# Expert down-projection: the 48-row pieces issued once for two pairs, and the two expert results of a token added by GpSimd

## The chip, the cores and the metric

The kernel runs on one core of one Trainium2 chip. The metric is the device time of one execution in microseconds (us), taken as the median of several runs. All data are fp32.

## What is computed

A transformer block on two sequences of 1024 tokens with 256 channels. First comes gated linear attention with 16 heads in chunks of 64 tokens. Then, on the layer-normed rows `xf`, comes a mixture of eight small experts with two picked for each token, plus a shared network:

```python
probs = softmax(xf @ gate_w.T); top_p, top_i = top_k(probs, 2)
combine = zeros(n, 8); combine[token, top_i] = top_p
h = silu(xf @ expert_fc1[e].T) * (xf @ expert_fc2[e].T)      # 176 hidden columns
y = sum over e of combine[:, e] * (h @ expert_proj[e].T)
shared = (silu(xf @ shared_fc1.T) * (xf @ shared_fc2.T)) @ shared_proj.T   # 704 hidden columns
y = y + sigmoid(xf @ shared_gate_w.T) * shared
out = x + gb * y
```

## The kernel before

Each engine has an instruction stream of its own, and semaphores tie the streams together. The attention runs over four blocks of 512 tokens (about the first 165 us). Then the routing is computed: every token's row is scattered to DRAM (`xs_dram`) twice, sorted by expert, so that each expert's rows fill tiles of 128. There are 39 such tiles (`ETILES`), numbered `i`, and they are handled in 20 pairs `q`. A group is eight tiles or four pairs (`EGRP`, `XPAIRS`); five groups are run, the middle three in a hardware loop.

For a pair, with `u` the tile's place in its group:

- SyncE (`load_tile`, L508) loads the rows into `xt`, which has a place for four pairs. It waits for the transposes of the tile that was there and for its row factors (`goal_ready`).
- The tensor engine (`group`, L1919) does for each even `u`: `up` of tile u (L1877), the transposes of a later tile's rows (`rows_T`, L1861), `hid_T` of the pair before (L1888, L1890), `up` and `rows_T` of tile u+1, and `down` of the pair before.
- `down` multiplies the 176 hidden columns as 128 plus 48. The 128-row parts are L1900. The 48-row part of the even tile sits in array rows 0 to 47 (L1902), that of the odd tile in rows 64 to 111 (L1907). The expert's 48 weight rows for the odd tile have first to be copied to that range by ScalarE (`copy_odd_rows`, L952, into `tail_odd`, two places). The result of tile t of a pair goes into columns 0 to 255 of the PSUM bank `work[t]`.
- The vector engine (`group`, L1419) multiplies the two halves of the hidden layer (`expert_h`, L1389), copies the transposed hidden columns to `hTe` (L1394), makes two row factors (`row_gains`, L1402) and takes the two results out of PSUM with their token weights (`evac_y`, L1409) into `yout`, which has a place for two pairs.
- GpSimd computes where each row goes (`goals`, L667 to L676, a chain of five small operations, two pairs ahead) and scatters the rows to `ys_dram` (`put_rows`, L684), where each token has two rows.

While the last tiles run, the tensor engine starts on the shared network of the last 512 tokens (`shared_up`, L1486 and L1478, then `shared_down`, L1501 and L1515). When all 39 scatters have landed, SyncE loads `ys_dram` back in eight transfers of 512 KB (L526, into `yin`, two for each block of 512 tokens). `combine(n)` on the vector engine then treats two tiles of tokens at a time: it adds the two results of each token (L1454) and adds the sum to `x_sb` (L1460 or L1458). Between these stand the products of the shared network (`mult_up`, L1130 and L1134). For the last four tiles `add_scaled_down` (L1150) adds the shared network's output. SyncE stores each finished tile.

Of the kernel before, what the change touches and what calls it, by code (L numbers as in the profile page):

```python
# [19 lines left out]
ALU = mybir.AluOpType  # L20
# [3 lines left out]
P = 128  # L24
# [153 lines left out]
def adaln_moe(nc, x, cT, wmod, wq, wk, wv, wg1, wg2, bg2, wgate, norm_w, wo,  # L178
              router, e_up, e_down, s_up, s_down, out):
    with ExitStack() as ctx:  # L180
# [40 lines left out]
        def part(n):  # L221
# [17 lines left out]
        tail_odd = xn2[:, 0:2, :]  # L239
# [100 lines left out]
        row_step, row_gain = sq[:, 0, 0:HID], sq[:, 1, :].rearrange("p (a n) -> p a n", a=2)  # L340
        yout = er_pos[:, :, :].rearrange("p a (t c) -> p a t c", t=2)
# [38 lines left out]
            sem("hTp_full"), sem("hTe_ready"), sem("down_full"), sem("y_out"), [sem(f"ys_st{i}") for i in range(4)])  # L380
# [3 lines left out]
        goal_ready, texp1_ready, odd_ready = sem("goal_ready"), sem("texp1_ready"), sem("odd_ready")  # L384
        ld_y = [sem(f"ld_y{i}") for i in range(NBLK)]
# [54 lines left out]
        def _(sp):  # L440
# [80 lines left out]
            for j, s in enumerate(ys_stored):  # L521
                sp.wait_ge(s, 16 * len(range(j, ETILES, 4)))
# [13 lines left out]
        def _(pool):  # L536
# [142 lines left out]
            def put_rows(q):  # L679

                for u in range(min(2, ETILES - 2 * q)):
                    i = 2 * q + u
                    pool.wait_ge(y_out, i + 1)
                    g.indirect_dma_start(out=ys_dram, out_offset=bass.IndirectOffsetOnAxis(ap=goal_u[:, i:i + 1], axis=0),  # L684
                                         in_=yout[:, q % 2, u, :], in_offset=None, bounds_check=TOPK * TOK - 1,
                                         oob_is_err=False).then_inc(ys_stored[i % 4], 16)
# [27 lines left out]
        def _(act):  # L714
# [231 lines left out]
            def odd_rows(q, w, e):  # L946

                act.wait_ge(down_full, q - 1)
                copy_odd_rows(w, e)

            def copy_odd_rows(w, e):
                a.activation(tail_odd[CHUNK:CHUNK + FE1, w % 2, :], edn[0:FE1, 0, bass.ds(e, 1), :].rearrange("p a n -> p (a n)"),  # L952
                             ACT.Copy).then_inc(odd_ready, 1)

            def group(i0, q0, tiles=EGRP, first=False, last=False):
                act.load(ereg, texp_u[0:1, bass.ds(i0, EGRP)])
                e = [act.snap(r, min_val=0, max_val=NE - 1) for r in ereg]
                for u in range(tiles):
                    expert_silu(i0 + u, u)
                    if u % 2:  # L960
                        if first and u < 4:
                            copy_odd_rows(u // 2, e[u])
                        else:
                            odd_rows(q0 + u // 2, u // 2, e[u])
                    if not (last and u + 2 >= tiles):
                        evac_rows(i0 + u + 2, u)

            group(0, 0, first=True)
            with act.Fori(1, ESLOTS // EGRP - 1) as grp:
                group(grp * EGRP, grp * XPAIRS)  # L970
            group(ESLOTS - EGRP, ESLOTS // 2 - XPAIRS, tiles=ETILES - ESLOTS + EGRP, last=True)
# [93 lines left out]
        def _(dve):  # L1065
# [330 lines left out]
            def row_gains(i, u):  # L1396

                if not isinstance(i, int) or i:
                    dve.wait_ge(y_out, i)
                dve.wait_ge(goal_ready, i + 2)  # L1400
                for t in range(2):
                    v.scalar_tensor_tensor(out=row_gain[:, t, :], in0=row_step, scalar=goal[:, (u // 2) % XPAIRS, t, 2:3],  # L1402
                                           in1=rows[:, 0, GB, :], op0=ALU.mult, op1=ALU.add).then_inc(gain_ready, 1)

            def evac_y(i0, q0, u):

                dve.wait_ge(down_full, q0 + u // 2 + 1)
                dve.wait_ge(gain_ready, i0 + u + 2 - u % 2)
                v.scalar_tensor_tensor(out=yout[:, (u // 2) % 2, u % 2, :], in0=work[u % 2][:, 0:HID],  # L1409
                                       scalar=goal[:, (u // 2) % XPAIRS, u % 2, 1:2], in1=row_gain[:, u % 2, :],  # L1410
                                       op0=ALU.mult, op1=ALU.mult).then_inc(y_out, 1)

            def y_slot_free(i0, u):

                n = 16 * (u // 4)
                if not isinstance(i0, int) or i0 or n:
                    dve.wait_ge(ys_stored[u % 4], i0 * 4 + n)

            def group(i0, q0, tiles=EGRP, first=False):  # L1419

                for u in range(0, tiles, 2):
                    expert_h(i0 + u, u)
                    if u or not first:
                        evac_hT(q0 + u // 2 - 1, (u // 2 - 1) % XPAIRS)
                        row_gains(i0 + u - 2 if u else i0 - 2, (u - 2) % EGRP)
# [13 lines left out]
            group(0, 0, first=True)  # L1439
            with dve.Fori(1, ESLOTS // EGRP - 1) as grp:  # L1440
                group(grp * EGRP, grp * XPAIRS)
            group(ESLOTS - EGRP, ESLOTS // 2 - XPAIRS, tiles=ETILES - ESLOTS + EGRP)
            evac_hT(EPAIRS - 1, XPAIRS - 1)
            row_gains(ETILES - 1, EGRP - 2)
            y_slot_free(ESLOTS - EGRP, EGRP - 2)
            evac_y(ESLOTS - EGRP, ESLOTS // 2 - XPAIRS, EGRP - 2)
# [75 lines left out]
        def _(pe):  # L1522
# [369 lines left out]
            def down(i, q, w, e, tiles=2):  # L1892

                pe.wait_ge(hTe_ready, q + 1)
                if isinstance(i, int) and i == 0:
                    pe.wait_ge(hs_ready, FTS * (NBLK - 1) + EARLY_UP)
                at_least(pe, y_out, i, 0)
                for t in range(tiles):
                    main = edn_odd if t else edn[:, 0, :, :]
                    t_.matmul(work[t][:, 0:HID], hTe[:, w % 2, t * P:(t + 1) * P],  # L1900
                              main[:, bass.ds(e[t], 1), :].rearrange("p a n -> p (a n)"), start=True, stop=False)
                ins = t_.matmul(work[0][:, 0:HID], hTe[0:FE1, w % 2, 2 * P:3 * P],  # L1902
                                edn[0:FE1, 1, bass.ds(e[0], 1), :].rearrange("p a n -> p (a n)"), start=False, stop=True)
                if tiles == 2:
                    pe.wait_ge(odd_ready, q + 1)
                    r = slice(CHUNK, CHUNK + FE1)
                    ins = t_.matmul(work[1][:, 0:HID], hTe[r, w % 2, 2 * P:3 * P], tail_odd[r, w % 2, :],  # L1907
                                    start=False, stop=True)
                ins.then_inc(down_full, 1)
# [7 lines left out]
            eprev = [pe.alloc_register(f"expert_prev{u}") for u in range(2)]  # L1917

            def group(i0, q0, before=None, tiles=EGRP, last=False):  # L1919
# [3 lines left out]
                def pair_behind(step, u):  # L1923
                    if u:
                        step(i0 + u - 2, q0 + u // 2 - 1, u // 2 - 1, e[u - 2:u])
                    elif before is not None:
                        step(i0 - 2, q0 - 1, XPAIRS - 1, before)

                for u in range(0, tiles, 2):
# [10 lines left out]
                    pair_behind(down, u)  # L1940
                    if u == 0:
                        for r, v_ in zip(eprev, e[-2:]):
# [23 lines left out]
            down(ETILES - 1, EPAIRS - 1, XPAIRS - 1, previous()[0:1], tiles=1)  # L1966
# [36 lines left out]
```

## Time and profile before

| | us |
|---|---|
| median of 3 runs | 374.45 (374.1 to 374.88) |
| the profiled execution, its own time | 373.3 |
| the profiled execution, its span (first to last instruction) | 371.5 |
| busy: tensor engine / weight loads | 360.9 / 226.3 |
| busy: vector engine / ScalarE / GpSimd | 238.1 / 144.0 / 146.7 |

The granted clock of the tensor engine is full over the whole span. A weight load is listed beside the matmuls because it overlaps them. fp32 matmuls appear as two records each, so a row with x4 stands for two of them. Idle time of an engine matters only where another one waits for it.

### The profile page before, as it was taken

What the parts mean: (1) busy time and instruction counts of PE and PEld (TensorE: products, weight loads), DVE (VectorE), ACT (ScalarE), POOL (GpSimd) and SP (SyncE); (2) the same over time, 40 slices, a digit from 0 to 9 for tenths busy, and PEclk for the clock granted to TensorE, in tenths of its full rate; (3) what the DMA queues carried; (4) which work ended last, traced back from release to release, by engine and by line L of the source; (5) the groups of instructions that cost most, each with busy time, mean ns of one, the idle gap of its engine ahead of it and who ended that gap; (6) DMA issues with size and microseconds to landing.
All of it is one profiled execution on the core that took longest, in us unless ns stands there. A gap on an engine that the chain in (4) does not pass through costs nothing.

```text
span 371.5 us, 10003 instructions
## 1 busy us (share of the span) xinstructions
PE 360.9 (97%) x3871; PEld 226.3 (61%) x3872; DVE 238.1 (64%) x578; ACT 144.0 (39%) x303; POOL 146.7 (39%) x253
## 2 busy tenths in 40 slices
PE   8999999999999989999999999999999999999996
PEld 8445656565766565647744844856666666665464
DVE  4199585998699579764591861165665555556386
ACT  3597638635781613180043311024333333331110
POOL 7706007100710242026270176323666677666200
PEclk9999999999999999999999999999999999999999
DMA  6980300000000000089820082422333333211396
GB/s 194 347 246 11 109 4 3 2 4 4 3 2 5 2 2 4 4 290 278 247 97 19 1 219 88 131 57 88 104 99 112 101 105 90 86 57 45 106 350 230
DMA packets 29901, 36.66 MB, mean 99 GB/s; under 512 B 4567, under 2 KB 26530, under 8 KB 29860
## 3 DMA queue, kind: packets, MB, share of 16 engines
q1 hardware_dynamic: 26452, 27.58, 24.9%
q0 software_dynamic: 3408, 8.51, 6.8%
q8 instruction: 29, 0.48, 0.5%
q14 instruction: 12, 0.10, 0.1%
HBM read 23.31 MB, written 13.68 MB: 100 GB/s over the span
## 4 chain that ended last, share of the span: by engine, by line
PE 87%; ACT 6%; DVE 3%; issue 2%; POOL 2%; DVEq 0%; POOLq 0%; ACTq 0%
PE at_ps L1877 13%; PE work L1486 10%; PE at_ps L1486 8%; PE work L1535 7%; PE at_ps L1501 6%; PE work L1900 5%; PE work L1501 4%; PE work L1902 3%; PE at_ps L1535 3%; PE work L1676 3%; PE at_ps L1861 2%; PE work L1726 2%; PE at_ps L1573 2%; PE o_even L1629 2%; PE at_ps L1726 2%
## 5 line engine op out<-in xcount | busy, mean ns | idle before, releaser
L684 POOL DMA_INDIRECT ys_tokens<-er_pos,goal_u x39 | 42.2, 1082 | 34.1 <-DVE er_pos L1409 26.7
L1877 PE MATMUL at_ps<-arena 128*128 x156 | 54.5, 472 | 0.0
L655 POOL DMA_INDIRECT xs_sorted<-h2tok,pos_u x32 | 31.4, 983 | 37.8 <-DVE pos_u L1031 17.0
L604 POOL TENSOR_TENSOR arena<-arena 128x512 f32<-128x512 f32 x8 | 10.2, 1281 | 76.0 <-DVE arena L1344 76.0
L1877 PEld LDWEIGHTS at_ps<-arena 128*128 128x128 f32 x156 | 26.6, 190 | 14.9 <-issue 6.6
L937 ACT ACTIVATE arena<-at_ps 128x176 f32<-128x176 f32 x39 | 12.4, 318 | 58.8 <-PE at_ps L1877 55.4
L1409 DVE SCALAR_TENSOR_TENSOR er_pos<-work,goal,sq 128x256 f32<-128x256 f32 x39 | 17.1, 480 | 22.0 <-PE work L1907 21.0
L1486 PE MATMUL work<-h2T,sup_sb 128*128 128x512 f32 x56 | 25.8, 600 | 0.2 <-ACT hs L705 0.2
L1389 DVE TENSOR_TENSOR arena<-at_ps,arena 128x176 f32<-128x176 f32 x39 | 13.3, 342 | 18.6 <-ACT arena L937 16.0
L1234 DVE COPY_PREDICATED arena<-causal,at_ps 128x512 f32<-128x512 uint32 x32 | 20.4, 720 | 4.0 <-PE at_ps L1573 4.0
L1501 PE MATMUL at_ps<-sdn_sb,hs 128*128 128x256 f32 x100 | 22.1, 380 | 0.0
L1501 PEld LDWEIGHTS at_ps<-sdn_sb,hs 128*128 128x128 f32 x100 | 18.9, 190 | 3.4 <-issue 1.0
L705 ACT ACTIVATE hs<-at_ps 128x512 f32<-128x512 f32 x9 | 5.4, 597 | 40.2 <-PE at_ps L1486 40.2
L1130 DVE TENSOR_TENSOR hs<-work,hs 128x512 f32<-128x512 f32 x12 | 8.3, 689 | 16.6 <-PE work L1486 16.5
L933 ACT ACTIVATE arena<-at_ps 128x256 f32<-128x256 f32 x39 | 14.9, 384 | 9.7 <-PE at_ps L1861 9.3
L616 POOL TENSOR_TENSOR sq<-sq,sg 128x512 f32<-128x512 f32 x8 | 10.0, 1275 | 21.7 <-issue 21.3
L1402 DVE SCALAR_TENSOR_TENSOR sq<-sq,goal,rows 128x256 f32<-128x256 f32 x40 | 17.4, 477 | 0.0
L1486 PEld LDWEIGHTS work<-h2T,sup_sb 128*128 128x128 f32 x56 | 10.2, 190 | 11.7 <-issue 11.2
L1861 PEld LDWEIGHTS at_ps<-ident,h2tok 128*128 128x128 f32 x78 | 10.9, 141 | 10.0 <-issue 6.1
L809 ACT ACTIVATE gate_pair<-gate_pair 128x512 f32<-128x512 f32 x8 | 4.9, 631 | 26.8 <-DVE gate_pair L1226 26.8
L1535 PE MATMUL work<-hT,wgate_sb 128*128 128x512 f32 x32 | 14.9, 602 | 0.0
L1861 PE MATMUL at_ps<-ident,h2tok 128*128 128x128 f32 x78 | 14.8, 273 | 0.0
(291 smaller groups left out, 823.1 us busy)
## 6 DMA issues: line engine op xcount, KB each, us to landing
h2tok<-xs_sorted SPq DMA_DIRECT2D x40, 131.5 KB
arena<-ys_tokens SPq DMA_DIRECT2D x8, 512.0 KB, 7.5
arena<-in_e_up SPq DMA_DIRECT2D x8, 352.0 KB
x_sb<-in_x SPq DMA_DIRECT2D x4, 512.0 KB, 8.6
out_rows<-x_sb SPq DMA_DIRECT2D x16, 128.0 KB, 3.9
sup_sb<-in_s_up SPq DMA_DIRECT2D x2, 640.0 KB, 4.9
xs_sorted<-state SPq DMA_DIRECT2D x2, 526.0 KB
xs_sorted<-state SPq DMA_DIRECT2D x8, 131.5 KB
```

The source lines that it names most:

```text
L655: g.indirect_dma_start(out=xs_dram, out_offset=bass.IndirectOffsetOnAxis(ap=pos_u[:, k, t:t + 1], axis=0), in_=h2tok[:, t, :], in_offset=N ...
L684: g.indirect_dma_start(out=ys_dram, out_offset=bass.IndirectOffsetOnAxis(ap=goal_u[:, i:i + 1], axis=0), in_=yout[:, q % 2, u, :], in_offs ...
L933: a.activation(xT[:, u % 2, :], at_ps[u % 2][:, 0:KC * P], ACT.Copy).then_inc(xT_ready, 1)
L1234: v.copy_predicated(atm[:, n % 2, j, :], causal[:, :, :].bitcast(U32).rearrange("p r l -> p (r l)"), at_ps[j][:, :]).then_inc(atm_ready, 1)
L1402: v.scalar_tensor_tensor(out=row_gain[:, t, :], in0=row_step, scalar=goal[:, (u // 2) % XPAIRS, t, 2:3], in1=rows[:, 0, GB, :], op0=ALU.mu ...
L1409: v.scalar_tensor_tensor(out=yout[:, (u // 2) % 2, u % 2, :], in0=work[u % 2][:, 0:HID], scalar=goal[:, (u // 2) % XPAIRS, u % 2, 1:2], in ...
L1486: ins = t_.matmul(o[0:m, :], sup_sb[:, k, w, f0:f0 + m], h2T_of[blk][:, k, :], start=(k == 0), stop=(k == KC - 1))
L1501: t_.matmul(o[jj][:, t * HID:(t + 1) * HID], hs[:, f, tk], sdn_sb[:, f, :], start=(t == 0 and f == 0), stop=False, skip_group_check=True)
L1535: ins = t_.matmul(o[:, :], w[:, k, gr * P:(gr + 1) * P], rhs[:, k, :], start=(k == 0), stop=(k == KC - 1))
L1861: ins = t_.transpose(at_ps[u % 2][:, k * P:(k + 1) * P], xt[:, u // 2, u % 2, k * P:(k + 1) * P], ident[:, :])
L1877: ins = t_.matmul(at_ps[2 + u % 2][:, 0:2 * FE], xT[:, u % 2, k * P:(k + 1) * P], eup[:, bass.ds(e, 1), k, :].rearrange("p a n -> p (a n)" ...
L1900: t_.matmul(work[t][:, 0:HID], hTe[:, w % 2, t * P:(t + 1) * P], main[:, bass.ds(e[t], 1), :].rearrange("p a n -> p (a n)"), start=True, s ...
```

## The change

The short matmuls leave `down` and get a function of their own, `down_short`, which issues those of two pairs (four tiles) after the second pair's `down`. To hold both pairs, `work[t]` is used over all 512 columns, the second pair in columns 256 to 511. `down_full` now counts blocks of two pairs. `tail_odd` gets four places. The vector engine takes four results out in one go (`out_rows`), and makes four row factors in one go in the cycle in between; `row_gain` moves to `xn` and has four places. `yout` gets four pairs' places, the additional ones in `h2T`, and each of the eight tiles has its own semaphore. GpSimd's `goals` runs three pairs ahead instead of two. At the end the eight additions of the tokens' two results (128x512 each) move from the vector engine to GpSimd, with a new semaphore `ysum_ready`. The vector engine's share of `combine` for n = 0 to 6 comes after the last product of the shared network, and `add_scaled_down(0)` comes ahead of the last `combine`.

```diff
-        tail_odd = xn2[:, 0:2, :]
+        tail_odd = xn2[:, :, :]
-        row_step, row_gain = sq[:, 0, 0:HID], sq[:, 1, :].rearrange("p (a n) -> p a n", a=2)
-        yout = er_pos[:, :, :].rearrange("p a (t c) -> p a t c", t=2)
+        row_step, row_gain = sq[:, 0, 0:HID], xn
+        yout = [home[:, a, :].rearrange("p (t c) -> p t c", t=2) for home in (er_pos, h2T[:, 0, :, :]) for a in range(2)]
...
-            goals(0)
-            goals(1)
+            for q in range(XPAIRS - 1):
+                goals(q)
             for q in range(EPAIRS):
-                if q + 2 < EPAIRS:
-                    goals(q + 2)
+                if q + XPAIRS - 1 < EPAIRS:
+                    goals(q + XPAIRS - 1)
                 put_rows(q)
+            for n in range(NTILE // 2):
+                if n % 2 == 0:
+                    pool.wait_ge(ld_y[2 * n // TPB], 16 * TOPK)
+                y0, y1 = (yin[:, 2 * n // TPB, k, 2 * n % TPB:2 * n % TPB + 2, :] for k in range(TOPK))
+                g.tensor_tensor(y0, y0, y1, ALU.add).then_inc(ysum_ready, 1)
...
-            def odd_rows(q, w, e):
-                act.wait_ge(down_full, q - 1)
+            def odd_rows(d, w, e):
+                act.wait_ge(down_full, d)
                 copy_odd_rows(w, e)
...
+            def out_rows(i0, d0, u, tiles=4):
+                for n in range(u, u + tiles):
+                    y_slot_free(i0, n)
+                    evac_y(i0, d0, n)
...
                     if u + 1 < tiles:
                         expert_h(i0 + u + 1, u + 1)
-                    for t in range(2):
-                        if u:
-                            y_slot_free(i0, u - 2 + t)
-                            evac_y(i0, q0, u - 2 + t)
-                        elif not first:
-                            y_slot_free(i0 - EGRP, EGRP - 2 + t)
-                            evac_y(i0 - EGRP, q0 - XPAIRS, EGRP - 2 + t)
+                    if u == 4:
+                        out_rows(i0, d0, 0)
+                    elif u == 0 and not first:
+                        out_rows(i0 - EGRP, d0 - XPAIRS // 2, 4)
+                    elif u % 4 == 2:
+                        row_gains(i0 + u - 2, u - 2)
+                        row_gains(i0 + u, u)
...
-                if n % 2 == 0:
-                    dve.wait_ge(ld_y[t // TPB], 16 * TOPK)
-                y0, y1 = (yin[:, t // TPB, k, t % TPB:t % TPB + 2, :] for k in range(TOPK))
-                steps.did(v.tensor_tensor(y0, y0, y1, ALU.add))
-                steps.sync()
+                dve.wait_ge(ysum_ready, n + 1)
+                y0 = yin[:, t // TPB, 0, t % TPB:t % TPB + 2, :]
...
-                for n in {3: (0,), 4: (1, 2, 3), 5: (4, 5, 6)}.get(f, ()):
+                for n in {5: (0, 1, 2, 3, 4, 5, 6)}.get(f, ()):
                     combine(n)
+            steps.sync()
+            add_scaled_down(0)
             combine(NTILE // 2 - 1)
             steps.sync()
-            for jj in range(2):
-                add_scaled_down(jj)
+            add_scaled_down(1)
...
-                at_least(pe, y_out, i, 0)
+                if w % 2 == 0:
+                    at_least(pe, y_out, i, 0)
+                c = slice(w % 2 * HID, w % 2 * HID + HID)
...
+            def down_short(q, w, e, tiles=4):
+                if tiles == 4:
+                    pe.wait_ge(odd_ready, q + 1)
+                else:
+                    pe.wait_ge(odd_ready, q)
+                r = slice(CHUNK, CHUNK + FE1)
+                for a in range(2):
+                    c = slice(a * HID, a * HID + HID)
+                    ins = t_.matmul(work[0][:, c], hTe[0:FE1, a, 2 * P:3 * P],
+                                    edn[0:FE1, 1, bass.ds(e[2 * a], 1), :].rearrange("p a n -> p (a n)"),
+                                    start=False, stop=True, skip_group_check=True)
+                    if 2 * a + 1 < tiles:
+                        ins = t_.matmul(work[1][:, c], hTe[r, a, 2 * P:3 * P], tail_odd[r, (w - 1 + a) % XPAIRS, :],
+                                        start=False, stop=True, skip_group_check=True)
+                ins.then_inc(down_full, 1)
...
                     pair_behind(down, u)
+                    short_behind(u)
```

## Rows read from the trace of the kernel before

**Rows 1.** The profile's busy table.
```profile
PE 360.9 (97%) x3871; PEld 226.3 (61%) x3872; DVE 238.1 (64%) x578; ACT 144.0 (39%) x303; POOL 146.7 (39%) x253
```
**Rows 2.** Chain of waits, one pair: start, us, engine, tile, line, records.
```profile
289.01 1.38 PE at_ps L1877 x4
...
290.94 1.19 PE at_ps L1877 x4
...
293.21 0.41 PE work L1902
293.63 0.21 PE work L1902
293.84 1.38 PE at_ps L1877 x4
```
**Rows 3.** Timeline, tensor engine, four short matmuls of the shared network and what follows.
```profile
178.60 1.14 PE L1515 MATMUL at_ps<-sdn_sb,hs 64*128 64x256 f32 x8
...
179.66 1.56 PE L1726 MATMUL work<-wo_sb,yT 128*128 128x256 f32 x6
```
**Rows 4.** Timeline of one pair: start, us, engine, line, out<-in, count [idle before, releaser].
```profile
289.12 0.88 DVE L1409 SCALAR_TENSOR_TENSOR er_pos<-work,goal,sq 128x256 f32<-128x256 f32 x2 [1.09 <-PE work L1907]
...
290.78 0.34 DVE L1389 TENSOR_TENSOR arena<-at_ps,arena 128x176 f32<-128x176 f32 x1 [0.79 <-ACT arena L937]
291.04 0.55 DVE L1394 COPY arena<-o_even 128x384 f32<-128x384 f32 x1
291.50 0.87 DVE L1402 SCALAR_TENSOR_TENSOR sq<-sq,goal,rows 128x256 f32<-128x256 f32 x2
...
292.18 0.60 PE L1900 MATMUL work<-arena 128*128 x2
...
292.51 0.34 DVE L1389 TENSOR_TENSOR arena<-at_ps,arena 128x176 f32<-128x176 f32 x1
```
**Rows 5.** Timeline, GpSimd: first scatter of pairs 0, 1 and 17.
```profile
256.60 1.10 POOL L684 DMA_INDIRECT ys_tokens<-er_pos,goal_u  x1 [12.11 <-DVE er_pos L1409]
...
261.41 1.09 POOL L684 DMA_INDIRECT ys_tokens<-er_pos,goal_u  x1 [0.83 <-DVE er_pos L1409]
...
339.02 1.09 POOL L684 DMA_INDIRECT ys_tokens<-er_pos,goal_u  x1 [0.78 <-POOL goal_u L676]
```
**Rows 6.** Timeline of the tail, all engines.
```profile
344.65 0.97 POOL L684 DMA_INDIRECT ys_tokens<-er_pos,goal_u  x1 [0.30 <-issue]
345.08 3.70 PE L1486 MATMUL at_ps<-hT,sup_sb 128*128 128x512 f32 x8
345.25 0.48 DVE L1409 SCALAR_TENSOR_TENSOR er_pos<-work,goal,sq 128x256 f32<-128x256 f32 x1 [1.01 <-PE work L1902]
...
346.51 0.97 POOL L684 DMA_INDIRECT ys_tokens<-er_pos,goal_u  x1 [0.88 <-issue]
...
354.26 0.69 DVE L1454 TENSOR_TENSOR arena<-arena 128x512 f32<-128x512 f32 x1 [1.25 <-DMA arena<-ys_tokens]
...
357.40 0.77 ACT L708 ACTIVATE hs<-at_ps 64x256 f32<-64x256 f32 x2 [2.84 <-PE at_ps L1478]
...
368.35 0.88 DVE L1150 SCALAR_TENSOR_TENSOR x_sb<-work,sgate,x_sb 128x256 f32<-128x256 f32 x2 [0.33 <-PE work L1515]
```
**Rows 7.** Timeline near 139 us; then three lines' durations (ns min/median/max).
```profile
139.24 1.35 POOL L633 TENSOR_TENSOR arena<-state,tmask 128x448 f32<-128x448 f32 x1 [4.70 <-DVE state L1287]
139.71 1.42 DVE L1264 TENSOR_TENSOR x_sb<-x_sb,tmp 128x512 f32<-128x512 f32 x1
140.67 0.67 POOL L639 TENSOR_TENSOR arena<-state,tmask 128x64 f32<-128x64 f32 x1
...
L1264 DVE TENSOR_TENSOR x_sb<-x_sb,tmp x8: 691/692/1423, 65.3 to 185.9; 128x512 f32<-128x512 f32 x8
...
L639 POOL TENSOR_TENSOR arena<-state,tmask x2: 347/509/671, 71.0 to 140.7; 128x64 f32<-128x64 f32 x2
...
L604 POOL TENSOR_TENSOR arena<-arena 128x512 f32<-128x512 f32 x8 | 10.2, 1281 | 76.0 <-DVE arena L1344 76.0
```

More of the change, by code:

```diff
@@ L379, in adaln_moe @@
         hTp_full, hTe_ready, down_full, y_out, ys_stored = (
-            sem("hTp_full"), sem("hTe_ready"), sem("down_full"), sem("y_out"), [sem(f"ys_st{i}") for i in range(4)])
+            sem("hTp_full"), sem("hTe_ready"), sem("down_full"), sem("y_out"), [sem(f"ys_st{i}") for i in range(EGRP)])
         weights_ready, row_ready, end_ready = sem("weights_ready"), sem("row_ready"), sem("end_ready")
@@ L521, in _ @@
             for j, s in enumerate(ys_stored):
-                sp.wait_ge(s, 16 * len(range(j, ETILES, 4)))
+                sp.wait_ge(s, 16 * len(range(j, ETILES, EGRP)))
             for q in range(NBLK):
@@ L944, in _, with group @@
             ereg = [act.alloc_register(f"odd_expert{u}") for u in range(EGRP)]
-            def odd_rows(q, w, e):
-                act.wait_ge(down_full, q - 1)
+            def odd_rows(d, w, e):
+                act.wait_ge(down_full, d)
                 copy_odd_rows(w, e)
             def copy_odd_rows(w, e):
-                a.activation(tail_odd[CHUNK:CHUNK + FE1, w % 2, :], edn[0:FE1, 0, bass.ds(e, 1), :].rearrange("p a n -> p (a n)"),
+                a.activation(tail_odd[CHUNK:CHUNK + FE1, w, :], edn[0:FE1, 0, bass.ds(e, 1), :].rearrange("p a n -> p (a n)"),
                              ACT.Copy).then_inc(odd_ready, 1)
-            def group(i0, q0, tiles=EGRP, first=False, last=False):
+            def group(i0, d0, tiles=EGRP, first=False, last=False):
                 act.load(ereg, texp_u[0:1, bass.ds(i0, EGRP)])
@@ L960, in group @@
                     if u % 2:
-                        if first and u < 4:
+                        if first:
                             copy_odd_rows(u // 2, e[u])
                         else:
-                            odd_rows(q0 + u // 2, u // 2, e[u])
+                            odd_rows(d0 + u // 4 - 1, u // 2, e[u])
                     if not (last and u + 2 >= tiles):
@@ L969, in _ @@
             with act.Fori(1, ESLOTS // EGRP - 1) as grp:
-                group(grp * EGRP, grp * XPAIRS)
-            group(ESLOTS - EGRP, ESLOTS // 2 - XPAIRS, tiles=ETILES - ESLOTS + EGRP, last=True)
+                group(grp * EGRP, grp * (XPAIRS // 2))
+            group(ESLOTS - EGRP, (ESLOTS // 2 - XPAIRS) // 2, tiles=ETILES - ESLOTS + EGRP, last=True)
             for f in range(EARLY_UP, FTS):
@@ L1396, in row_gains @@
             def row_gains(i, u):
-                if not isinstance(i, int) or i:
+                if u % 4 == 0 and (not isinstance(i, int) or i):
                     dve.wait_ge(y_out, i)
@@ L1401, in row_gains, with evac_y, group @@
                 for t in range(2):
-                    v.scalar_tensor_tensor(out=row_gain[:, t, :], in0=row_step, scalar=goal[:, (u // 2) % XPAIRS, t, 2:3],
+                    v.scalar_tensor_tensor(out=row_gain[:, u % 4 + t, :], in0=row_step, scalar=goal[:, (u // 2) % XPAIRS, t, 2:3],
                                            in1=rows[:, 0, GB, :], op0=ALU.mult, op1=ALU.add).then_inc(gain_ready, 1)
-            def evac_y(i0, q0, u):
-                dve.wait_ge(down_full, q0 + u // 2 + 1)
+            def evac_y(i0, d0, u):
+                dve.wait_ge(down_full, d0 + u // 4 + 1)
                 dve.wait_ge(gain_ready, i0 + u + 2 - u % 2)
-                v.scalar_tensor_tensor(out=yout[:, (u // 2) % 2, u % 2, :], in0=work[u % 2][:, 0:HID],
-                                       scalar=goal[:, (u // 2) % XPAIRS, u % 2, 1:2], in1=row_gain[:, u % 2, :],
+                c = slice((u // 2) % 2 * HID, (u // 2) % 2 * HID + HID)
+                v.scalar_tensor_tensor(out=yout[(u // 2) % 4][:, u % 2, :], in0=work[u % 2][:, c],
+                                       scalar=goal[:, (u // 2) % XPAIRS, u % 2, 1:2], in1=row_gain[:, u % 4, :],
                                        op0=ALU.mult, op1=ALU.mult).then_inc(y_out, 1)
             def y_slot_free(i0, u):
[L1415 to L1419, printed above, removed]
+                if not isinstance(i0, int) or i0:
+                    dve.wait_ge(ys_stored[u], i0 * (16 // EGRP))
+            def out_rows(i0, d0, u, tiles=4):
+                for n in range(u, u + tiles):
+                    y_slot_free(i0, n)
+                    evac_y(i0, d0, n)
+            def group(i0, q0, d0, tiles=EGRP, first=False):
                 for u in range(0, tiles, 2):
@@ L1438, in _ @@
             steps.sync()
-            group(0, 0, first=True)
+            group(0, 0, 0, first=True)
             with dve.Fori(1, ESLOTS // EGRP - 1) as grp:
-                group(grp * EGRP, grp * XPAIRS)
-            group(ESLOTS - EGRP, ESLOTS // 2 - XPAIRS, tiles=ETILES - ESLOTS + EGRP)
+                group(grp * EGRP, grp * XPAIRS, grp * (XPAIRS // 2))
+            group(ESLOTS - EGRP, ESLOTS // 2 - XPAIRS, (ESLOTS // 2 - XPAIRS) // 2, tiles=ETILES - ESLOTS + EGRP)
             evac_hT(EPAIRS - 1, XPAIRS - 1)
-            row_gains(ETILES - 1, EGRP - 2)
-            y_slot_free(ESLOTS - EGRP, EGRP - 2)
-            evac_y(ESLOTS - EGRP, ESLOTS // 2 - XPAIRS, EGRP - 2)
+            out_rows(ESLOTS - EGRP, (ESLOTS // 2 - XPAIRS) // 2, 4, tiles=3)
             def combine(n):
                 t = 2 * n
-                if n % 2 == 0:
-                    dve.wait_ge(ld_y[t // TPB], 16 * TOPK)
-                y0, y1 = (yin[:, t // TPB, k, t % TPB:t % TPB + 2, :] for k in range(TOPK))
-                steps.did(v.tensor_tensor(y0, y0, y1, ALU.add))
-                steps.sync()
+                dve.wait_ge(ysum_ready, n + 1)
+                y0 = yin[:, t // TPB, 0, t % TPB:t % TPB + 2, :]
                 xv = x_sb[:, t:t + 2, :]
@@ L1896, in down @@
                     pe.wait_ge(hs_ready, FTS * (NBLK - 1) + EARLY_UP)
-                at_least(pe, y_out, i, 0)
+                if w % 2 == 0:
+                    at_least(pe, y_out, i, 0)
+                c = slice(w % 2 * HID, w % 2 * HID + HID)
                 for t in range(tiles):
                     main = edn_odd if t else edn[:, 0, :, :]
[L1900 to L1904, printed above, removed]
-                    pe.wait_ge(odd_ready, q + 1)
-                    r = slice(CHUNK, CHUNK + FE1)
-                    ins = t_.matmul(work[1][:, 0:HID], hTe[r, w % 2, 2 * P:3 * P], tail_odd[r, w % 2, :],
-                                    start=False, stop=True)
+                    t_.matmul(work[t][:, c], hTe[:, w % 2, t * P:(t + 1) * P],
+                              main[:, bass.ds(e[t], 1), :].rearrange("p a n -> p (a n)"),
+                              start=(w % 2 == 0), stop=False, skip_group_check=True)
+            def down_short(q, w, e, tiles=4):
+                if tiles == 4:
+                    pe.wait_ge(odd_ready, q + 1)
+                else:
[9 more added lines that the diff above has]
+                                        start=False, stop=True, skip_group_check=True)
                 ins.then_inc(down_full, 1)
@@ L1915, in fetch_experts @@
                 pe.load(ereg, texp_u[0:1, bass.ds(i0, EGRP)])
-            eprev = [pe.alloc_register(f"expert_prev{u}") for u in range(2)]
+            eprev = [pe.alloc_register(f"expert_prev{u}") for u in range(4)]
             def group(i0, q0, before=None, tiles=EGRP, last=False):
@@ L1926, in pair_behind, with short_behind @@
                     elif before is not None:
-                        step(i0 - 2, q0 - 1, XPAIRS - 1, before)
+                        step(i0 - 2, q0 - 1, XPAIRS - 1, before[2:4])
+                def short_behind(u):
+                    if u == 4:
+                        down_short(q0 + 1, 1, e[0:4])
+                    elif u == 0 and before is not None:
+                        down_short(q0 - 1, XPAIRS - 1, before)
                 for u in range(0, tiles, 2):
@@ L1940, in group @@
                     pair_behind(down, u)
+                    short_behind(u)
                     if u == 0:
-                        for r, v_ in zip(eprev, e[-2:]):
+                        for r, v_ in zip(eprev, e[-4:]):
                             pe.reg_mov(r, v_)
@@ L1965, in _ @@
             shared_up(pe, t_, begin, NBLK - 1, EARLY_UP, kinds=("SB",))
-            down(ETILES - 1, EPAIRS - 1, XPAIRS - 1, previous()[0:1], tiles=1)
+            down(ETILES - 1, EPAIRS - 1, XPAIRS - 1, previous()[2:3], tiles=1)
+            down_short(EPAIRS - 1, XPAIRS - 1, previous(), tiles=3)
             shared_up(pe, t_, begin, NBLK - 1, EARLY_UP + 1)
```

6 lines of the change are left out of this document (3 added, 3 removed).

## Prediction

> **What bounds the kernel now.** I read the busy table first: the tensor engine works 97% of the span [rows 1]. Then the chain of waits in order of time. In the expert stage it is tensor engine from end to end, and one pair of tiles takes 4.83 us (from 289.01 to 293.84) [rows 2]. Then the timelines of the vector engine and of GpSimd in that stage [rows 4, 5], since both get new duties, and the timeline of the last 30 us [rows 6]. There the vector engine closes the kernel: its last instruction runs from 368.35 to 369.23, and the last store fills the rest of the 371.5 us. Last I looked for a stretch in which GpSimd and the vector engine both add from SBUF, because the change makes them do so at the end [rows 7].
>
> **The short pieces.** A pair pays for its 48-row matmuls three times. The chain shows 0.41 and 0.21 us for them, and the next `up` takes 1.38 us where the `up` that follows a transpose takes 1.19 [rows 2]: 0.62 + 0.19 = 0.81 us a pair. Four short matmuls on two alternating row ranges stand elsewhere in the trace: from the start of L1515 to the start of the next matmul is 1.06 us [rows 3], against 0.62 for two, so a second pair adds 0.44. Done once for two pairs: 0.81 + 0.44 = 1.25 in place of 1.62, 0.37 to 0.38 less. There are 20 pairs, so ten such blocks (the last has three matmuls in place of four and saves the same): 3.8 us of tensor work, with no wait in front of it. I take it whole.
>
> **The vector engine in the loop.** A cycle without short pieces lasts 4.83 - 0.81 = 4.02 us, one with them 5.27. The four outputs come in a row: two take 0.88, four 1.75, so from a start like 289.12 they end at 290.87, 0.09 later than the next multiplication begins now (290.78). The copy of hTe, 291.04 plus 0.55, ends near 291.7, and the matmul that needs it starts at 292.18 [rows 4]: 0.5 us of cover, cost nothing. If it were gone, each tenth beyond it would cost a tenth in ten cycles. The four row factors (1.74 us) follow the second multiplication (292.51 plus 0.34), end at 294.6, and the next cycle's first multiplication comes at 290.78 + 4.02 = 294.80: it fits with 0.2. Behind them on this engine stand only that multiplication and the hTe copy. The ScalarE copies for odd tiles have four places in place of two and wait for an older block; they cost nothing. The load queue of SyncE still waits for the row factors of a pair before it loads the one four pairs on; those come at about their old time, since they are queued behind one scatter less but the scatters start later.
>
> **GpSimd in the loop.** Same work for a pair: two scatters and a chain of five small operations. What it needs for that is not plain. Between the first two pairs 4.81 us pass with a gap of 0.83, in the later one of 0.78, so a turn takes 4.76; over 16 pairs the mean is (339.02 - 261.41)/16 = 4.85 [rows 5]. GpSimd is as full as the tensor engine. The first scatter now waits for the first block: 256.60 + 4.83 - 0.38 = 261.05 in place of 256.60. The scatters of pair 16 then start at 261.05 + 16 turns; four scatters of 1.40 (1.10 plus 0.30) later GpSimd is free for tile 36: at 342.8 with 4.76, at 344.25 with 4.85. The tensor engine would give it tile 36 at 345.08 - 3.8 + 0.17 + 0.48 + 0.78 = 342.7 [rows 6]. I take a turn of 4.77, since nothing but its own work paced the first: 343.0. The new places for eight tiles of output (eight semaphores) keep this backlog away from the vector engine.
>
> **The tail.** After tile 36 two more scatters are queued, 1.27 each (0.97 plus 0.30), so the last starts at 343.0 + 2.54 = 345.5, where it stood at 346.51. From the last scatter to the first sum 7.75 us passed (354.26) [rows 6]; the loads are the same, so the first results land at 353.3. The 3.8 us of the loop have become 1.0 here, because the last block hands over three tiles at once and GpSimd takes them one by one.
>
> Then GpSimd makes the eight sums. One 128x512 addition takes it 1.28 us, the vector engine 0.68 to 0.69 [rows 6, 7]. The decisive rows are at 139 us. L1264 on the vector engine, two SBUF inputs of the very shape of the final addition, is given 1.42 us where it normally has 0.69: it starts at 139.71 inside GpSimd's L633 (139.24 to 140.59) and ends at 141.13, 0.54 us after GpSimd let go. And GpSimd's next, L639, takes 0.67 where the other has 0.35: it ends at 141.34, 0.21 us after the vector engine [rows 7]. Each stood still for the other. So the additions take turns. The vector engine has 0.54 of each turn, GpSimd 1.28 less the 0.14 of L639 that lay under the wait (0.35 - 0.21), which gives 1.68, or with nothing hidden 1.82. I take the middle, 1.75. The Trainium skill ("SBUF — State Buffer", Who interferes with whom) says that a Vector instruction with two SBUF inputs and a GpSimd one that reads SBUF contend, and that the first holds the port for its whole instruction, the other blocking fully. By whole instructions a turn would be 1.28 + 0.69 = 1.97, by the rows it is 1.68 to 1.82; the sum goes by the rows.
>
> The vector engine is free for its additions when it has done the last product: the ScalarE part ends at 358.17, less 3.8 is 354.4, and two halves of 256 columns take it 0.88 (as at 368.35), which is 355.3 (the two sums that used to stand ahead of it are gone). By then GpSimd is in its second sum, 353.3 + 2 x 1.28 = 355.9. Six turns follow: 355.9 + 10.5 = 366.4. Then what is left, alone: addition 0.54, product onto the output 0.88, addition 0.69, product 0.88, with two waits between them of 0.1, in all 3.2: 369.6. Before it was 369.23. The tensor engine ends at 364.5 and waits for nobody. **Sum:** 0.4 us more; span 371.9, its own time 373.7 in place of 373.3. The profiled execution lies 1.15 below the median of the runs shown; I set the difference against the median: 374.85.
>
> **The rivals.** (1) No turns at the end: only L1264 in one place speaks for them with this shape, and if they cost nothing, GpSimd is ready at 353.3 + 10.2 = 363.5, the last addition and product at 365.3, and the tensor engine with 364.5 + 0.1 + 0.88 = 365.5 decides: 3.75 faster, 370.7. Against it stand both directions in rows 7. (2) Half of it: the turns overlap by more than 0.14 because requests come at other phases; at 1.45 a turn the end is 367.8, 1.4 faster, 373.05. (3) The slower one: GpSimd falls behind in the loop. At 4.85 a pair tile 36 starts at 344.25, the results land at 354.5, and all else follows, 1.2 later than in the forecast: 1.6 slower, 376.05. It passes 0.75 us from 4.80 a pair on. For it speaks the mean over 16 pairs, against it that the tensor engine's own 4.83 may have paced that mean. (4) Turns of whole instructions, 1.97, as the skill's page states them: with the last alone 0.15 more, 1.5 more than the forecast, 1.9 slower, 376.3; the 0.54 speaks against it. (5) The loop doesn't give the 3.8 because the hTe copy comes late: the tail is bound by GpSimd's additions, so up to about 1 us of it would be seen nowhere, the rest as in (3).
>
> **How the numbers follow.** Forecast 0.46, with a range of its own of 374.2 (turn 1.68, landing 353.1) to 375.5 (turn 1.82, landing 353.5); (1) 0.16, (2) 0.08, (3) with (5) 0.22, (4) 0.08. Range 373.0 to 376.4: it holds (2), (3) and (4) and leaves out (1) and tails. A measurement here tells about 0.2%, 0.75 us. Faster by more 0.24, within 0.42 (nearly all of the forecast's case), slower 0.34 (cases 3 and 4 and the upper edge of the forecast's).
>
> **What would show it.** Four `down` short matmuls in a row every 9.28 us, and the last one ending near 341.3. The last scatter near 345.5, the first GpSimd sum near 353.3. Additions of the vector engine that read 1.1 to 1.2 us in place of 0.69, GpSimd's sums starting 1.7 to 1.8 apart, the tensor engine done 4 to 5 us before the last product. If vector additions read 0.69 beside GpSimd sums, I am wrong by rival 1; if the last scatter is at 346.5 or later, by rival 3.

## The result, and the profile after

The changed kernel takes 376.63 us (median of 6 runs, 376.1 to 377.79), the kernel before 374.38 us (6 runs) beside it: the ratio is 1.0063 (95% interval 1.0043 to 1.0082), 2.25 us slower. I had forecast 0.4 us slower and a range that ends at 376.4.

The two profiled executions differ by more, 376.0 against 371.5 us of span, and this must be cleared first. The instructions of the first 240 us are the same in both. The granted clock is not, as the view of stretches shows (us, then busy time and number for each engine, last the granted clock, the DMA share and GB/s), first before, then after:

```profile
10.00:15.00 5.00, 4.42 (x21) 1.48 (x19) 0.00 (x0) 1.64 (x3) 4.94 (x3) 1.00 1.01 359
```

```profile
10.00:15.00 5.00, 5.00 (x21) 2.01 (x19) 0.00 (x0) 1.61 (x3) 4.94 (x3) 0.72 1.00 352
```

For part of these five us the clock stood at 1.2 instead of 2.4 GHz: taken in stretches of one us, the granted clock is 0.50 from 10 to 12 us after, and 1.00 before. At the first product behind it that has `wq`, the changed kernel is 0.93 us late (timeline of PE, before and after):

```profile
22.04 1.88 PE L1535 MATMUL at_ps<-hT,wq_sb 128*128 128x512 f32 x4
```

```profile
22.97 1.88 PE L1542 MATMUL at_ps<-hT,wq_sb 128*128 128x512 f32 x4
```

The first `up` of the expert stage, at 247.42 before, comes at 249.59 after: 2.17 us of the difference lie ahead of everything that was changed. 0.93 of it is there at 22 us, the other 1.24 comes up in small steps of the stages between, and I did not find its cause. Both come and go with the execution: of the seven experiments below, e1, e2, e6 and e7 show the fall of the clock, e3, e4 and e5 have 1.00 there; e5, without it, still has its first `up` at 248.73; and the runs of the kernel before itself spread from 373.3 to 377.6 us. So I don't put it down to the change. From here on, times of different traces are compared from their first `up`:

| us after the first `up` | before | forecast | after |
|---|---|---|---|
| last short matmul of the loop over | 97.7 | 93.9 | 93.8 |
| first scatter | 9.2 | 13.6 | 13.6 |
| last scatter | 99.1 | 98.1 | 99.5 |
| first sum of the two results | 106.8 | 105.9 | 107.6 |
| last vector instruction over | 121.8 | 122.2 | 123.3 |
| end of the span | 124.1 | 124.5 | 126.4 |

The chain of the changed kernel, in order of time, for one block of two pairs. It answers to [rows 2]:

```profile
298.96 1.38 PE at_ps L1884 x4
...
302.29 0.86 PE work L1909 x4
303.16 1.18 PE at_ps L1884 x4
...
306.29 0.87 PE work L1909 x4
307.16 0.41 PE work L1922
307.57 0.21 PE work L1922
307.79 0.21 PE work L1922
308.01 0.21 PE work L1922
308.22 1.38 PE at_ps L1884 x4
```

The short matmuls (L1922) stand once for two pairs, the `up` in the middle takes 1.18 and no longer 1.38, and the block takes 308.22 - 298.96 = 9.26 us, where two pairs took 9.66. The loop gains 3.8 us, as forecast. But at the end the chain leaves the tensor engine:

```profile
349.12 0.98 POOL L685 DMA_INDIRECT ys_tokens<-h2T,goal_u  x1 [0.30 <-issue]
...
357.20 2.49 POOL L699 TENSOR_TENSOR arena<-arena 128x512 f32<-128x512 f32 x2 [7.10 <-DMA arena<-ys_tokens]
358.57 2.27 DVE L1466 TENSOR_TENSOR x_sb<-arena,x_sb 128x512 f32<-128x512 f32 x2 [1.15 <-POOL arena L699]
...
360.21 9.68 POOL L699 TENSOR_TENSOR arena<-arena 128x512 f32<-128x512 f32 x6 [0.52 <-DMA arena<-ys_tokens]
...
362.07 6.69 DVE L1466 TENSOR_TENSOR x_sb<-arena,x_sb 128x512 f32<-128x512 f32 x4 [1.23 <-POOL arena L699]
365.53 1.13 PE L1522 MATMUL work<-sdn_sb,hs 64*128 64x256 f32 x4
368.69 1.75 DVE L1464 TENSOR_TENSOR x_sb<-arena,x_sb 128x512 f32<-128x512 f32 x1
370.47 0.88 DVE L1156 SCALAR_TENSOR_TENSOR x_sb<-work,sgate,x_sb 128x256 f32<-128x256 f32 x2
...
371.98 0.88 DVE L1156 SCALAR_TENSOR_TENSOR x_sb<-work,sgate,x_sb 128x256 f32<-128x256 f32 x2
```

This is the timeline of the tail, beside [rows 6]. The tensor engine is done at 366.7, 6.2 us before the last product of `add_scaled_down` ends. Six sums of GpSimd take 9.68 us. One of them begins while the vector engine is idle and takes 1.26, the others run beside additions and take 1.66 to 1.76 (1.28 alone, [rows 7]). Four additions of the vector engine take 6.69, 1.67 each instead of 0.69: they take turns. The durations of the two lines (ns, min/median/max) say the same:

```profile
L699 POOL TENSOR_TENSOR arena<-arena x8: 1262/1682/1757, 357.2 to 368.2; 128x512 f32<-128x512 f32 x8
...
L1466 DVE TENSOR_TENSOR x_sb<-arena,x_sb x6: 677/1710/1753, 358.6 to 367.0; 128x512 f32<-128x512 f32 x6
```

The last scatter has not moved forward at all (99.5 against 99.1), although the last block was ready 3.8 us earlier.

Why is it late? The same timeline around GpSimd's last chain of small operations, with the row factors of the vector engine (L1408):

```profile
338.27 0.88 DVE L1408 SCALAR_TENSOR_TENSOR xn<-sq,goal,rows 128x256 f32<-128x256 f32 x2
338.42 0.88 POOL L668 TENSOR_SCALAR second<-h2tok,texp 128x1 f32<-128x1 f32 x2
...
339.96 0.88 DVE L1408 SCALAR_TENSOR_TENSOR xn<-sq,goal,rows 128x256 f32<-128x256 f32 x2 [0.81 <-POOL goal L674]
...
340.02 0.52 POOL L677 TENSOR_SCALAR goal_u<-goal 128x2 uint32<-128x2 f32 x1
```

L668 takes 0.88 us for two where it mostly takes 0.58, and L677 0.52 where it mostly takes 0.23. Both fall under row factors, which read two wide SBUF inputs. Under L1416, whose one wide input comes from PSUM and the other from SBUF, the same L668 keeps its 0.58:

```profile
280.41 1.66 DVE L1416 SCALAR_TENSOR_TENSOR er_pos<-work,goal,xn 128x256 f32<-128x256 f32 x4 [1.47 <-issue]
...
280.83 0.58 POOL L668 TENSOR_SCALAR second<-h2tok,texp 128x1 f32<-128x1 f32 x2
```

From the first scatter of pair 0 to that of pair 16, 263.23 to 341.31, the mean turn is 4.88 us:

```profile
263.23 1.09 POOL L685 DMA_INDIRECT ys_tokens<-er_pos,goal_u  x1 [14.82 <-DVE er_pos L1416]
...
278.43 1.09 POOL L685 DMA_INDIRECT ys_tokens<-h2T,goal_u  x1 [0.78 <-POOL goal_u L677]
...
283.14 1.09 POOL L685 DMA_INDIRECT ys_tokens<-er_pos,goal_u  x1 [0.78 <-POOL goal_u L677]
...
341.31 1.09 POOL L685 DMA_INDIRECT ys_tokens<-er_pos,goal_u  x1 [0.78 <-POOL goal_u L677]
```

An undisturbed turn is there too, 278.43 to 283.14: 4.71. Seven of the sixteen turns are 4.71, the others 4.81 to 5.30. Behind pair 0 only pair 2 still waits for its results, 0.3 us; for all later ones up to pair 16 the releaser is GpSimd's own L677. The tensor engine now needs 9.26 / 2 = 4.63 us a pair, so GpSimd runs without a pause and falls behind.

### The profile page after: what moved, and what is told of

Its sections match the earlier page's. It is cut to its first block, busy times and chain, and to the rows that moved or that the text cites. A ratio compares the mean times of both kernels' runs of the same rounds, so it can differ in the third digit from the quotient of the medians.

```text
span 376.0 us, 9991 instructions
## 1 busy us (share of the span) xinstructions
PE 358.9 (95%) x3871; PEld 228.6 (61%) x3872; DVE 237.9 (63%) x570; ACT 144.1 (38%) x303; POOL 159.5 (42%) x261
## 4 chain that ended last, share of the span: by engine, by line
PE 76%; ACT 5%; DVE 5%; issue 5%; DMA 4%; POOL 4%; SPq 1%; DVEq 0%; POOLq 0%
PE at_ps L1884 12%; PE work L1493 9%; PE work L1542 7%; PE at_ps L1508 6%; PE at_ps L1493 5%; PE work L1909 4%; PE at_ps L1542 3%; PE work L1683 3%; PE work L1922 2%; PE at_ps L1868 2%; PE work L1733 2%; DMA arena<-ys_tokens 2%; PE o_even L1636 2%; PE at_ps L1580 2%; PE at_ps L1733 2%
## 5 line engine op out<-in xcount | busy, mean ns | idle before, releaser
L1884 PE MATMUL at_ps<-arena 128*128 x156 | 53.7, 466 | 0.0
L605 POOL TENSOR_TENSOR arena<-arena 128x512 f32<-128x512 f32 x8 | 10.2, 1282 | 77.9 <-DVE arena L1350 77.9
L685 POOL DMA_INDIRECT ys_tokens<-er_pos,goal_u x20 | 20.9, 1044 | 24.4 <-DVE er_pos L1416 14.8
L685 POOL DMA_INDIRECT ys_tokens<-h2T,goal_u x19 | 19.9, 1045 | 9.9 <-POOL goal_u L677 5.4
L1408 DVE SCALAR_TENSOR_TENSOR xn<-sq,goal,rows 128x256 f32<-128x256 f32 x40 | 16.8, 480 | 0.8 <-POOL goal L674 0.8
L668 POOL TENSOR_SCALAR second<-h2tok,texp 128x1 f32<-128x1 f32 x40 | 13.1, 351 | 5.8 <-DMA h2tok<-xs_sorted 5.2
L699 POOL TENSOR_TENSOR arena<-arena 128x512 f32<-128x512 f32 x8 | 12.1, 1543 | 7.6 <-DMA arena<-ys_tokens 7.6
```

The lines of the kernel that those rows point to most:

```text
L1408: v.scalar_tensor_tensor(out=row_gain[:, u % 4 + t, :], in0=row_step, scalar=goal[:, (u // 2) % XPAIRS, t, 2:3], in1=rows[:, 0, GB, :], op ...
L1884: ins = t_.matmul(at_ps[2 + u % 2][:, 0:2 * FE], xT[:, u % 2, k * P:(k + 1) * P], eup[:, bass.ds(e, 1), k, :].rearrange("p a n -> p (a n)" ...
```

## The experiments

Theory A: two costs eat the 3.8 us and more, the backlog of GpSimd's scatters and the turns of the additions. The rivals took one of them away or named another cause. Each ratio is against runs of the kernel before on the same chip, and the us given with it are worked out from it. The two medians can give somewhat other us, so the sizes of single costs are read from the traces.

**e1: the sums back on the vector engine.**

```diff
-            for n in range(NTILE // 2):
-                ...
-                g.tensor_tensor(y0, y0, y1, ALU.add).then_inc(ysum_ready, 1)
 def combine(n):
-                dve.wait_ge(ysum_ready, n + 1)
+                if n % 2 == 0:
+                    dve.wait_ge(ld_y[t // TPB], 16 * TOPK)
+                steps.did(v.tensor_tensor(y0, y0, y1, ALU.add))
+                steps.sync()
```

> The changed kernel, with the eight 128x512 sums of the two results made by the vector engine again, all behind the last product of the shared network. Theory A (two costs: GpSimd's scatters come late, and the additions take turns): the landing of the results stays where the changed kernel has it, but from there to the last product the vector engine alone needs 8 x 1.40 + 2 x 0.9 = 13.0 us in place of the 15.7 measured, so 2.5 us faster than the changed kernel: 374.1, level with before. Theory B (the turns cost nothing, all of the loss is the late scatters): no faster than the changed kernel, 376.6.

Measured: ratio 0.9969 (0.9943 to 0.9995), 1.2 us faster than before. That it is faster at all is weakly shown: the medians, 373.59 and 373.84, are 0.25 us apart. That it is faster than the changed kernel is not in doubt. The timeline, vector engine:

```profile
357.42 0.69 DVE L1458 TENSOR_TENSOR arena<-arena 128x512 f32<-128x512 f32 x1
358.21 0.69 DVE L1464 TENSOR_TENSOR x_sb<-arena,x_sb 128x512 f32<-128x512 f32 x1
358.82 0.68 DVE L1458 TENSOR_TENSOR arena<-arena 128x512 f32<-128x512 f32 x1
...
369.49 0.88 DVE L1151 SCALAR_TENSOR_TENSOR x_sb<-work,sgate,x_sb 128x256 f32<-128x256 f32 x2
```

Both additions for two tiles take it 1.40 us (357.42 to 358.82). With GpSimd making one of the two, a step took 1.67. So in the changed kernel half of this work was taken away from the vector engine, and it became slower. Its work behind its last product takes 12.95 us here (357.42 to 370.37), 13.0 expected. The last scatter is as late as in the changed kernel (99.5 after the first `up`), the last vector instruction ends at 120.8 in place of 123.3. Theory B falls.

**e2 and e7: the sums on GpSimd alone, in the kernel before.** The diff of the tail, without the rest of the change.

```diff
+            for n in range(NTILE // 2):
+                ...
+                g.tensor_tensor(y0, y0, y1, ALU.add).then_inc(ysum_ready, 1)
-                for n in {3: (0,), 4: (1, 2, 3), 5: (4, 5, 6)}.get(f, ()):
+                for n in {5: (0, 1, 2, 3, 4, 5, 6)}.get(f, ()):
```

> The kernel before, with only the end of the change: the sums on GpSimd and the vector engine's part in the new order. Theory A: the landing stays at 354.3, the end takes 15.7 in place of 15.0 us, so 0.7 us slower than before, 375.1, and the vector additions read 1.1 to 1.3 us beside GpSimd's sums. Theory C (the additions account for the whole loss): 2 us slower, 376.5. Theory B: at 375.4 or less with additions of 0.69.

Measured: ratio 1.0054 (1.0030 to 1.0078), 2.0 us slower. That is more than theory A gave it and as much as theory C. In the trace GpSimd waits 2.15 us for the second block of results. Whether this belongs to the kernel, a second trace of it shows.

> The same kernel as e2_adds_only, for a second trace: there GpSimd waited 2.15 us between its second and third sum for the second block of results, where the changed kernel waits 0.52, and this wait made the loss 2 us in place of 0.7. If it belongs to this order of work, the gap is 2 us again; if it is chance of one transfer, it is near 0.5.

One execution, 376.79 us. The same kernel has a gap of 0.50 here, so the 2.15 does not belong to the kernel:

```profile
356.10 2.49 POOL L699 TENSOR_TENSOR arena<-arena 128x512 f32<-128x512 f32 x2 [6.71 <-DMA arena<-ys_tokens]
359.10 2.49 POOL L699 TENSOR_TENSOR arena<-arena 128x512 f32<-128x512 f32 x2 [0.50 <-DMA arena<-ys_tokens]
```

But the loss stays: 1.6 us of span from the first `up`. The timeline says why my 0.7 was too small (the vector engine, then GpSimd's last four sums):

```profile
360.11 0.87 DVE L1140 TENSOR_TENSOR hs<-at_ps,hs 64x256 f32<-64x256 f32 x2 [1.75 <-ACT hs L714]
361.01 8.43 DVE L1463 TENSOR_TENSOR x_sb<-arena,x_sb 128x512 f32<-128x512 f32 x6
...
362.13 6.76 POOL L699 TENSOR_TENSOR arena<-arena 128x512 f32<-128x512 f32 x4 [0.54 <-DMA arena<-ys_tokens]
```

In this kernel the last product ends only at 361.0, 4.9 us after the landing, and the vector engine has to put off all of its additions until then; before, it began them when the results landed. Putting them off would not cost anything by itself: six additions at 0.69 would be over near 365.2 (an estimate), and the tensor engine works until 370.2. But GpSimd's last four sums then still run beside them, 1.69 each, and the six take 8.43. I had carried over the 15.7 us of the changed kernel, where the wait is 0.2. So the part "sums on GpSimd, all additions last" costs 1.6 to 2 us where the loop is the old one. It doesn't add up with the others: in the changed kernel the last product is 3.8 us earlier, and so the order costs nearly nothing there.

**e3: no row factors in the loop.** The computation is changed: each row gets the first batch's gain.

```diff
-                    v.scalar_tensor_tensor(out=row_gain[:, u % 4 + t, :], in0=row_step, scalar=goal[...], in1=rows[:, 0, GB, :], ...
+                    v.tensor_copy(row_gain[:, u % 4 + t, 0:1], rows[:, 0, GB, 0:1]).then_inc(gain_ready, 1)
...
+            for n in range(4):
+                steps.did(v.tensor_copy(row_gain[:, n, :], rows[:, 0, GB, :]))
```

> The changed kernel without the row factors in the expert loop (each is replaced by a copy of one column; the batch's own factor is left out of the result), so that the vector engine has no instruction with two SBUF inputs there. Theory A says that GpSimd's 4.88 us a pair are its own 4.71 plus waits for the port that the row factors hold: the turn falls to 4.71, the last scatter comes 1.7 us earlier (then bound by the tensor engine), total 1.7 less than the changed kernel, 374.9. Theory D (the scatters are slowed by other DMA traffic or by the order of the waits): the turn stays at 4.8 to 4.9 and the time at 376.6.

Measured: ratio 1.0038 (1.0011 to 1.0065). GpSimd's turn falls to (339.29 - 263.51)/16 = 4.74 us, fourteen of the sixteen to 4.70:

```profile
263.51 1.08 POOL L685 DMA_INDIRECT ys_tokens<-er_pos,goal_u  x1 [14.85 <-DVE er_pos L1415]
...
339.29 1.09 POOL L685 DMA_INDIRECT ys_tokens<-er_pos,goal_u  x1 [0.78 <-POOL goal_u L677]
```

So the row factors do hold GpSimd up, and theory D falls. The time fell by less than expected, about 1 us: the four copies that I put ahead of the loop kept the tensor engine waiting 0.73 us for the first tile's hidden layer, and every scatter with it. The last scatter came 0.9 us earlier than in the changed kernel, not 1.7.

**e4: the row targets of two pairs in one chain.** GpSimd's two chains of five small operations between the scatters become one of seven behind them.

```diff
 def goals(q):
+                a = slice(q % XPAIRS, q % XPAIRS + 2)
...
-                steps.did(g.tensor_tensor(turned[:, slot, :, :], xt[:, slot, :, X_TURN:X_NONE + 1], ...
+                steps.did(g.tensor_tensor(turned[:, a, :, :], xt[:, a, :, X_TURN:X_NONE + 1], ...
...
-            for q in range(XPAIRS - 1):
-                goals(q)
+            goals(0)
+            goals(2)
             for q in range(EPAIRS):
-                if q + XPAIRS - 1 < EPAIRS:
-                    goals(q + XPAIRS - 1)
                 put_rows(q)
+                if q % 2 and q + 3 < EPAIRS:
+                    goals(q + 3)
```

> The changed kernel, with the row targets of two pairs computed in one chain of seven small operations on GpSimd, behind the four scatters of a block, in place of two chains of five between them. GpSimd then has about 4.2 us a pair to do and waits for the blocks. Theory A: the last scatter is bound by the tensor engine, 1.4 to 1.7 us earlier, total 374.9 to 375.2. If the lateness of the scatters is no part of the loss, 376.6.

Measured: ratio 1.0023 (0.9996 to 1.0049), 0.9 us above before, which the interval doesn't tell from none, and some 1.5 below the changed kernel. GpSimd now waits for each block and the last scatters follow the tensor engine:

```profile
343.05 0.97 POOL L688 DMA_INDIRECT ys_tokens<-h2T,goal_u  x1 [2.71 <-DVE h2T L1419]
344.33 0.97 POOL L688 DMA_INDIRECT ys_tokens<-h2T,goal_u  x1 [0.30 <-issue]
345.61 0.97 POOL L688 DMA_INDIRECT ys_tokens<-h2T,goal_u  x1 [0.31 <-issue]
```

The last is at 97.7 after the first `up` (345.61 less 247.90), 1.8 us earlier than in the changed kernel, and the last vector instruction 2.1 earlier. The backlog is the second cost, and theory C, by which the additions are the whole loss, falls.

**e5: both repairs.** e1 and e4 together.

> Both repairs: the row targets of two pairs in one chain, and the sums back on the vector engine, all behind the last product. The results land 2 us earlier than in e1_adds_back, but there the vector engine began its additions the moment it was free, so its own work (8 x 1.40 + 2 x 0.9) is the bound. Theory A: within 0.3 us of e1_adds_back, 373.4 to 373.8 at the same level of before. Theory E (the landing of the results bounds the end in every version): 1.5 to 2 us faster than e1_adds_back, 372.

Measured: ratio 0.9958 (0.9937 to 0.9978). From the first `up` to the last vector instruction it takes 120.7 us, e1 120.8. The last scatter starts 1.8 us earlier than in e1 (97.7 against 99.5) and it changes nothing: the vector engine has no gap between its last product and the end. Theory E falls.

**e6: both repairs, and the first additions in the vector engine's idle time.**

```diff
-                for n in {5: (0, 1, 2, 3, 4, 5, 6)}.get(f, ()):
+                for n in {4: (0,), 5: (1, 2, 3, 4, 5, 6)}.get(f, ()):
```

> As e5_joint_back, with the vector engine's first pair of additions ahead of the last product of the shared network, where it has been idle for 1.75 us and where the results have just landed (5.5 us before that in the clean trace of the joint chain: 353.4 against 354.75). Theory A: the idle time takes the 1.4 us of work, so 1.3 us faster than e5_joint_back and about 2.3 us faster than the kernel before, 371.7 to 372.3. If the landing comes a little too late the gain shrinks to 0.5.

Measured: ratio 0.9935 (0.9912 to 0.9958), 372.49 us against 374.86 of the kernel before beside it, 2.4 us faster. This version beats both kernels.

```profile
354.77 0.69 DVE L1461 TENSOR_TENSOR arena<-arena 128x512 f32<-128x512 f32 x1 [0.63 <-DMA arena<-ys_tokens]
355.57 0.69 DVE L1467 TENSOR_TENSOR x_sb<-arena,x_sb 128x512 f32<-128x512 f32 x1
356.29 0.87 DVE L1138 TENSOR_TENSOR hs<-at_ps,hs 64x256 f32<-64x256 f32 x2
```

The expectation's "5.5 us before that" is a slip: from 353.4 to 354.75 it is 1.3 us. The first pair begins when the results land, and the last product (L1138) follows without a gap. The last vector instruction ends 119.7 after the first `up`, 1.0 earlier than in e5. The tensor engine ends at 366.0, still 2.8 us before it. So of the 3.8 us of the loop 2.1 come through, and the vector engine, which is busy from the landing to its end (354.77 to 368.76, 14.0 us), holds the rest.

## Why the prediction was wrong, point by point

**The short pieces and the loop.** Right. 3.8 us forecast, 97.66 - 93.84 = 3.8 measured, and the vector engine never kept the tensor engine waiting.

**The first scatter.** Right, 13.6 after the first `up` in both.

**GpSimd's turn.** This is the step that failed: "I take a turn of 4.77, since nothing but its own work paced the first". It measured 4.88. Over 16 pairs that is 1.75 us, of which 1.4 were left at the last scatter, because its last scatters ran with 1.28 where I had counted 1.40. I had the rule for it in hand. [Rows 7] showed the engines blocking each other, and I used them only for the end. The row factors have two SBUF inputs as well, and four of them now come in a row, while GpSimd, which hardly waits for anything any more, has small operations that read SBUF under way. Pair 2's wait for its block is 0.3 of the 1.75. e3 shows the cause and e4 the price. My rival 3 is what came: it named the backlog, on top of the forecast's own turns at the end, put the edge at 4.80 a pair and gave 376.05 for 4.85. Its sign, a last scatter at 346.5 or later, is there: 99.5 after the first `up` is 346.9 in the time of the trace before.

**The landing.** 8.1 us after the last scatter instead of 7.75; a spread that transfers have here, as the 0.5 to 2.15 us between first and second block in e2 and e7.

**The turns at the end.** The mechanism held in both directions, the size was a little less than forecast. Where both engines alternate, an addition follows the other after 1.67 us: the 1.68 that the rows gave with 0.14 hidden, and not the middle of 1.75 that I took. One of the six sums began while the vector engine was idle and took 1.26. Against that stand 0.52 us for a transfer that was not in the sum. From the landing to the end of the last vector instruction it takes 15.7 us, forecast 16.3. The sign I named, additions that read 1.1 to 1.2 us, was wrong: beside a sum an addition reads 1.67 to 1.75, a whole turn. The Trainium skill ("SBUF — State Buffer", Who interferes with whom) calls the contention an exclusive lock, and says of the vector engine's two-port modes that the one that comes first holds the port for its whole instruction. Read so for two SBUF inputs, a turn would have been 1.97; who blocks whom agrees with the traces, the size, 1.67, does not. Rival 1, no turns, is refuted by e1: taking GpSimd out made the end faster by 2.4 us.

**The close.** Not in the sum at all. After the last vector instruction the kernel before ends 2.3 us later, the changed one 3.1. The queue's own waits show where 0.8 of it is, first before, then after:

```profile
SPq L180 <- PEq L180: 0.2, 1, 0.2
```

```profile
SPq L180 <- PEq L180: 1.0, 1, 1.0
```

SyncE waits for the tensor engine's sequencer at the closing barrier, in the changed kernel, e3 and e4 for 1.0 us, in before, e1, e5 and e6 for 0.2. In the three with 1.0 the tensor engine had long been idle and its granted clock was at half. But that holds for e1 and e5 as well, and their wait is 0.2. What makes this wait long stays open.

**The sum.** Forecast 0.4 us slower; backlog and landing add 1.7, the shorter turns, less the 0.52 for the transfer, take 0.6 back, the close adds 0.8: 2.3, against 2.3 in the traces from the first `up` and 2.25 in the medians. The direction was right, the range (to 376.4) ended 0.2 us too low. Rival 3 held backlog and turns together, but with 4.85 and not 4.88, and no case had the close. The backlog's 1.4 alone or the close's 0.8 alone would have left the median inside the range.

## What to carry to other kernels

Work moved to GpSimd is not moved away from the vector engine if both read from SBUF with two-input instructions: here a shared step took 1.67 us where the vector engine alone did both halves in 1.40. Look for such pairs over the whole kernel and not only where the diff puts one, and count an engine's load by its own undisturbed turn against the turn it must keep: one that is 2% over even so (here 4.71 against 4.63) will hand its backlog to whatever waits for its last result. And a gain in the loop is worth only what the tail lets through; ask first what the tail will be bound by once the loop is shorter.

## What the runs showed of the hardware that I had not expected

A GpSimd operation of 128x2 elements takes 0.52 instead of 0.23 us when it falls under a vector instruction with two SBUF inputs: 0.3 us more, where a 128x512 sum pays 0.4 beside an addition (1.67 instead of 1.28). The granted clock fell to half in the first 15 us of five of the nine executions traced and not of the other four, though the kernels have the same instructions there. The changed kernel's trace was 0.93 us late at 22 us, and with what came up later it was 2.17 us late at the first `up`, nearly as much as the change is worth. The wait at the closing barrier took 0.2, 0.4 or 1.0 us; it was 0.4 in both traces of the one kernel that was traced twice (e2 and e7).
